# Attention computed head by head with 1024-column exponentials, in place of pairs of heads with 512-column ones

## The reference, cut to what matters

```python
xh  = x.reshape(b, c, h, he).transpose(0, 2, 1, 3)      # c = 2048 tokens, h = 16, he = 64
qkv = einsum('bhce,ef->bhcf', xh, Wqkv) + bqkv
q, k, v = split(qkv, 3, axis=-1)
att = einsum('bhqe,bhke->bhqk', q, k) / sqrt(he)
mask = tril(ones((c, c)), k=-1)
att = softmax(att * mask, axis=-1)      # masked scores are 0, not -inf: they count as exp(0) = 1
out = einsum('bhqk,bhke->bhqe', att, v)
x = x + (out @ Wr + br)                 # x was layer-normed before attention
x = x + moe(layernorm(x))               # 1 shared + 8 routed experts, D=1024, H=2048
```

## Time and profile before

| | us |
|---|---|
| two timed runs | 4086.95 and 4326.6, median 4206.77 |
| the profiled run's own time | 4113.86 |
| its span, slowest core (core 3) | 4112.3 |
| its span, fastest core (core 0) | 3973.3 |
| TensorE busy on core 3 | 3071.2 (75%) |
| DVE busy | 1200.4 (29%) |
| ACT busy | 869.4 (21%) |

### The profile page before, as it was taken

How to read it: one execution, slowest core, us unless ns; L and a number is a source line. 1 busy time by engine, 2 the same in 40 slices (tenths; PEclk the granted TensorE clock), 3 DMA queues, 4 the chain that set the end, 5 groups by cost and what they waited for, 6 DMA issues and landing times.

```text
span 4112.3 us, 45933 instructions; the slowest of 8 cores (3973.3 to 4112.3 us)
## 1 busy us (share of the span) xinstructions
PE 3071.2 (75%) x15380; PEld 1367.7 (33%) x15380; DVE 1200.4 (29%) x2450; ACT 869.4 (21%) x1354; POOL 29.2 (1%) x55
## 2 busy tenths in 40 slices
PE   2354445554545445837999999999999999999997
PEld 0122222222222222313444444344444444444343
DVE  5222222222222222361132323223332232323222
ACT  0232323232323223002211121211212211121210
POOL 0000000000000000000000000000000000000000
PEclk7555555555555555868988999889998888999888
DMA  2100000000000000040040222204022040222202
GB/s 83 26 1 1 1 1 1 1 1 1 1 1 1 1 1 1 1 83 1 11 72 1 41 42 42 42 1 83 1 41 42 11 72 1 42 42 42 42 1 82
DMA packets 7087, 98.28 MB, mean 24 GB/s; under 512 B 1860, under 2 KB 2260, under 8 KB 2388
## 3 DMA queue, kind: packets, MB, share of 16 engines
q0 software_dynamic: 3984, 77.81, 11.2%
q1 hardware_dynamic: 2884, 17.53, 1.3%
HBM read 164.58 MB, written 8.39 MB: 42 GB/s over the span
## 4 chain that ended last, share of the span: by engine, by line
PE 68%; DVE 13%; ACT 8%; issue 8%; DMA 1%; DVEq 1%; ACTq 0%; SPq 0%; POOL 0%
PE PM L771 27%; PE PM L860 26%; PE PS L460 6%; DVE SMASK L433 4%; PE PS L409 3%; ACT PTE L422 3%; ACT PTO L439 2%; ACT PTE L439 2%; PE PTR L492 2%; DVE AVN L485 2%; PE PS L533 1%; DVE RZ L480 1%; PE PS L383 1%; PE PS L374 1%; DVE TMPLN L243 1%
## 5 line engine op out<-in xcount | busy, mean ns | idle before, releaser
L771 PE MATMUL PM<-XLN,W 128*128 128x512 bf16 x4608 | 1100.3, 406 | 0.7 <-DVE WSB L729 0.7
L860 PE MATMUL PM<-H1G,W 128*128 128x512 bf16 x4608 | 1058.9, 395 | 0.0
L788 ACT ACTIVATE H1G<-PM,B1C 128x512 bf16<-128x512 f32 x576 | 395.9, 687 | 1750.9 <-PE PM L771 1750.9
L771 PEld LDWEIGHTS PM<-XLN,W 128*128 128x128 bf16 x4608 | 473.8, 103 | 623.6 <-issue 304.7
L860 PEld LDWEIGHTS PM<-H1G,W 128*128 128x128 bf16 x4608 | 464.9, 101 | 589.5 <-issue 196.9
L409 PE MATMUL PS<-QT,KT 64*128 64x512 bf16 x640 | 345.0, 582 | 258.5 <-DVE SMASK L433 171.5
L837 DVE TENSOR_TENSOR H1G<-H1G,WB 128x512 bf16<-128x512 bf16 x512 | 217.7, 425 | 765.7 <-ACT H1G L788 765.7
L875 DVE TENSOR_TENSOR XRES<-XRES,PM 128x512 f32<-128x512 f32 x288 | 198.2, 688 | 709.5 <-PE PM L860 709.5
L492 PE MATMUL PTR<-IDB,AVN 128*64 128x128 bf16 x256 | 68.8, 269 | 351.3 <-DVE AVN L485 351.3
L433 DVE TENSOR_TENSOR SMASK<-PS,MASKS 128x512 f32<-128x512 f32 x256 | 177.1, 692 | 480.4 <-PE PS L409 378.2
L409 PEld LDWEIGHTS PS<-QT,KT 64*128 64x128 bf16 x640 | 64.9, 101 | 526.8 <-issue 520.5
(11 more groups left out here) (102 smaller groups left out, 1149.0 us busy)
## 6 DMA issues: line engine op xcount, KB each, us to landing
W<-w1cat POOLq DMA_DIRECT2D x9, 4096.0 KB, 28.6
W<-w2cat POOLq DMA_DIRECT2D x9, 4096.0 KB, 28.5
XRES<-xt SPq DMA_DIRECT2D x8, 1024.0 KB
ot<-XRES SPq DMA_DIRECT2D x8, 1024.0 KB
WRF<-wr_rl POOLq DMA_DIRECT2D x1, 2048.0 KB, 17.0
MASKS<-c_masks SPq DMA_DIRECT2D x1, 512.0 KB
B1C<-b1col POOLq DMA_DIRECT2D x9, 8.0 KB, 27.9
B2C<-b2col_t POOLq DMA_DIRECT2D x9, 4.0 KB, 3.2
```

The costliest lines, as they stand in the source:

```text
L771: lambda e, psv=psv, kc=kc, ht=ht, tt=tt: e.matmul(psv, W1[:, kc * DFF + ht * 128: kc * DFF + (ht + 1) * 128], xln(kc)[:, tt * 512:(tt + 1 ...
L788: lambda e, h1sl=h1sl, psv=psv, e_i=e_i, ht=ht: e.activation(h1sl, psv, AF.Gelu, bias=B1C[:, (e_i % 2) * 16 + ht: (e_i % 2) * 16 + ht + 1]),
L860: lambda e, psv=psv, kc=kc, dtl=dtl, buf=buf: e.matmul(psv, W2[:, kc * D + dtl * 128: kc * D + (dtl + 1) * 128], H1G[:, buf * 8192 + kc * 512:
```

## The change

Each head is now worked on by itself.

- Q and K: one 64-row matmul and one eviction for each slot, in four banks of PS4; a matmul of the third and fourth token tile waits for the eviction two tiles before it. QT and KT have 64 partitions, VA one head. Every head lies in partitions 0 to 63 of QT and KT.
- V: as before for one head; its first matmul waits for PS2, which Q and K no longer use. The first score matmul waits for the Q/K evictions only, the AV matmuls for the copy of V.
- Unmasked scores: two key tiles of one head fill two neighbouring banks, and one exponential reads 1024 columns. Its event goes to `sc_hist` twice.
- Masked scores: two masks, each 512 columns, fill both halves of SMASK, both after the preceding exponential; one exponential of 1024 columns follows. Each mask's event goes to `sc_hist`.
- AV: once for each head and block, then the same four steps, but reciprocal and scaling read PS1 in PSUM; the copy to PAVS is gone. PS1 comes free with the last copy into AVT.
- The mask constant is float32 and so twice as large.

```diff
-    c_masks = dt("c_masks", [128, 4 * 512], BF16, kind="ExternalInput").ap()
+    c_masks = dt("c_masks", [128, 4 * 512], F32, kind="ExternalInput").ap()
...
-                for hp in range((min(H, DBG["nheads"]) + 1) // 2):
...
+                for h in range(min(H, DBG["nheads"])):
+                    ch, off = h // 2, (h % 2) * 64
...
+                            if s >= 2:
+                                w = [("SS", evs[s - 2])]
+                            else:
+                                w = [slot_free[slot_id]]
...
+                            tq = P.emit("tensor",
+                                        lambda e, psv=psv, wcol=wcol, tsl=tsl, xh=xh,
+                                        off=off: e.matmul(
+                                            psv, WQ[off:off + 64, wcol:wcol + 64],
+                                            xh[:, tsl],
+                                            start=True, stop=True),
+                                        waits=w, inc="ST")
...
+                        for kc0 in range(0, 4 * j, 2):
+                            slot = rot % 6
+                            rot += 2
...
+                            for q in range(2):
+                                kc = kc0 + q
+                                psv = base[:, boff + q * 512: boff + (q + 1) * 512]
+                                w = [slot_free[slot + q]]
                                 if len(sc_hist) >= 2:
                                     w.append(sc_hist[-2])
...
+                            ss_exp_last = P.emit("scalar",
+                                    lambda e, base=base, boff=boff, kc0=kc0: e.activation(
+                                        PT[:, kc0 * 512:(kc0 + 2) * 512],
+                                        base[:, boff:boff + 1024],
+                                        AF.Exp, scale=0.125),
+                                    waits=[("ST", ts)] + ptguard, inc="SS")
+                            slot_free[slot] = ("SS", ss_exp_last)
+                            slot_free[slot + 1] = ("SS", ss_exp_last)
+                            sc_hist.append(("SS", ss_exp_last))
+                            sc_hist.append(("SS", ss_exp_last))
+                        for kc0 in range(4 * j, 4 * j + 4, 2):
...
+                                vm = P.emit("vector",
+                                        lambda e, psv=psv, d=d, q=q: e.tensor_mul(
+                                            SMASK[:, q * 512:(q + 1) * 512],
+                                            psv, MASKS[:, d * 512:(d + 1) * 512]),
+                                        waits=[("ST", ts), ("SQ", sq_masks),
+                                               ("SS", ss_exp_last)], inc="SV")
+                                slot_free[slot + q] = ("SV", vm)
+                                sc_hist.append(("SV", vm))
...
+                            ss_exp_last = P.emit("scalar",
+                                    lambda e, kc0=kc0: e.activation(
+                                        PT[:, kc0 * 512:(kc0 + 2) * 512],
+                                        SMASK[:, 0:1024],
+                                        AF.Exp, scale=0.125),
+                                    waits=[("SV", vm)] + ptguard, inc="SS")
...
-                            pcp = P.emit("vector",
-                                    lambda e: e.tensor_copy(PAVS[:, 0:260], PS1[:, 0:260]),
-                                    waits=[("ST", st_av), ("SV", ps1_free[1])], inc="SV")
-                            ps1_free = ("SV", pcp)
...
+                                        RZ[:, mt:mt + 1],
+                                        PS1[:, mt * 65 + 64: mt * 65 + 65]),
...
+                                        AVN[:, mt * 64:(mt + 1) * 64],
+                                        PS1[:, mt * 65: mt * 65 + 64],
+                                        RZ[:, mt:mt + 1], None, ALU.mult),
...
+                        ps1_free = ("SV", avt_done)
```

More of the change, by code:

```diff
@@ L315, in build_program @@
                 avt_done = 0
[L317 to L322, removed]
-                for hp in range((min(H, DBG["nheads"]) + 1) // 2):
[L325 to L336, removed]
-                                w += [("SV", ln1_done), ("GQ", gq_wq)]
[L338 to L392, removed]
@@ L393, in build_program @@
                                        PS2.ap().rearrange("p (g n) -> p g n", n=64)),
                                    waits=[("ST", tv_last), ("SV", sv_vones)], inc="SV")
-                        ps2_free = ("SV", sv_va[oh])
-                    for j in range(NTT):
[L397 to L403, removed]
+                    else:
+                        sv_va = sv_vones
@@ new lines, in build_program @@
+                                            KT[0:64, kc * 128:(kc + 1) * 128],
+                                            QT[0:64, j * 512:(j + 1) * 512],
+                                            start=True, stop=True),
+                                        waits=w, inc="ST") or ts
+                            ptguard = [("ST", st_av_prev)] if kc0 == 0 else []
+                            ss_exp_last = P.emit("scalar",
[4 more added lines that the diff above has]
+                                    waits=[("ST", ts)] + ptguard, inc="SS")
@@ new lines, in build_program @@
+                            slot_free[slot] = ("SS", ss_exp_last)
[3 more added lines that the diff above has]
+                        for kc0 in range(4 * j, 4 * j + 4, 2):
+                            slot = rot % 6
+                            rot += 2
+                            base = (PS4 if slot < 4 else PS2)
+                            boff = (slot if slot < 4 else slot - 4) * 512
+                            vm = 0
+                            for q in range(2):
+                                kc = kc0 + q
+                                psv = base[:, boff + q * 512: boff + (q + 1) * 512]
+                                w = [slot_free[slot + q]]
+                                if len(sc_hist) >= 2:
+                                    w.append(sc_hist[-2])
+                                if kc == 0 and j == 0:
+                                    w += [("SS", ev_q[-1]), ("SS", ev_k[-1])]
+                                ts = P.emit("tensor",
+                                        lambda e, psv=psv, kc=kc, j=j: e.matmul(
+                                            psv,
+                                            KT[0:64, kc * 128:(kc + 1) * 128],
+                                            QT[0:64, j * 512:(j + 1) * 512],
+                                            start=True, stop=True),
+                                        waits=w, inc="ST")
+                                d = kc - 4 * j
+                                vm = P.emit("vector",
[6 more added lines that the diff above has]
+                                sc_hist.append(("SV", vm))
+                            ptguard = [("ST", st_av_prev)] if kc0 == 0 else []
+                            ss_exp_last = P.emit("scalar",
[4 more added lines that the diff above has]
+                                    waits=[("SV", vm)] + ptguard, inc="SS")
@@ new lines, in build_program @@
+                        st_av = 0
+                        for mt in range(4):
+                            for kc in range(16):
+                                if kc < 4 * j + 4:
+                                    lhs = PT[:, kc * 512 + mt * 128: kc * 512 + (mt + 1) * 128]
+                                else:
+                                    lhs = ONES[:, 0:128]
+                                w = []
+                                if mt == 0 and kc == 0:
+                                    w = [("SS", ss_exp_last), ("SV", sv_va), ps1_free]
+                                st_av = P.emit("tensor",
+                                        lambda e, lhs=lhs, mt=mt, kc=kc: e.matmul(
+                                            PS1[:, mt * 65:(mt + 1) * 65],
+                                            lhs, VA[:, kc * 65:(kc + 1) * 65],
+                                            start=(mt == 0 and kc == 0), stop=(kc == 15),
+                                            skip_group_check=True),
+                                        waits=w,
+                                        inc=("ST" if (mt == 3 and kc == 15) else None)) or st_av
@@ L514, in build_program @@
+                        ps1_free = ("SV", avt_done)
+                        if h == 0 and j == 0:
+                            _DBGREF["PT"] = PT
+                            _DBGREF["AVN"] = AVN
+                            _ckpt("j0")
                 _DBGREF["AVT"] = AVT
```

204 lines of the change are left out of this document (93 added, 111 removed).

## The result

The changed kernel takes 4182.6 us (median of 11 runs), the kernel before 4130.3 (10 runs). Some executions are held back on part of the cores by a lower clock; the ratio of those that aren't is 1.0194, with a 95% interval from 1.0105 to 1.0283. So after is slower, by about what was summed (1.8%): the interval excludes 1, but leaves open whether it is more or less than 2%. The profiled execution of after took 4128.1 us, its slowest core 4126.6.

A forecast was written before the change was run, and what follows sets the result against it. Attention was taken as a chain with one engine working at a time, so its length counts. Terms of +98, -26 and +2 gave +74 us on 4112.3, then 1.6 for the profiled run: 4188 us, range 4135 to 4250.

The forecast's parts named there:

- Unmasked cycle: Unmasked scores: two matmuls, then one 1024-column exponential, 2.28 us against 1.42 before; 192 pairs, +165 us.
- Masked pair: Masked scores: two masks, then one exponential, 2.56 us against 3.04 before; 128 pairs, -61 us.
- Both with Q/K/V: Q/K/V and all score blocks: 61.9 us per head, 990 us for 16 heads against 892 before, +98 us.
- Normalisation: After AV: dropping the copy to PAVS saves 34 us, less the cost of PSUM reads; -26 us.
- Loading the masks: Start of kernel: masks load as 1024 KB, not 512, beside the WRF load before the first Q matmul; +2 us.
- The rival of dear PSUM reads: Normalisation: reads from PSUM 65 ns slower eat 33 of the 34 us saved; 4213 us, chance 0.15.
- The clock rival: Score blocks: clock rises to 2.4 GHz, a cycle loses 0.39 us; no change, about 4113 us, chance 0.05.
- The other rivals: Slower matmuls and masks, no copy saving, up to 4258 us (0.10); TensorE a pair ahead, 3950 (0.04); chain unlengthened, 4115 (0.04).
- The sign: Whole kernel: chances of slower 0.45, faster 0.04, within 2% 0.51, with 82 us taken as the measurable limit.

The follow-up runs named there:

- e3: Changed kernel with unmasked exponentials of 512 columns again, one per matmul, each with its own history entry; attention 1445.6 us, 165.1 less than the changed kernel.
- e6: Changed kernel with masked items one by one again (mask, 512-column exponential, next mask waits); attention 1675.2 us, 64.5 more than the changed kernel.
- e4: Changed kernel with one history entry, not two, for each unmasked exponential; attention 1408.1 us, 202.6 less than the changed kernel.
- e7: Changed kernel with the mask in bf16 again; attention 1611.4 us against 1610.7, first Q matmul at 129.1 us against 130.9.
- e1: Changed kernel with score matmuls waiting only for their banks, not the history list; attention 1373.2 us.
- e9: The changed kernel itself again, five rounds beside the kernel before; ratio 1.0125, from 1.0033 to 1.0218.

## Why the prediction was right, and where it was wrong

**The time and its mechanism: right.** 4188 us were predicted, 4182.6 measured. That the two lie within 6 us is in part luck: the executions of after lie at 4128, 4155, 4183 and above, by what clock the expert part got, and attention grew by 66 us where the sum has 72 for it. Step by step:

- *Unmasked cycle.* 0.43 + 0.68 + 1.03 + 0.14 = 2.28 us; measured 2.27. The exponential of 1024 columns takes 1.024 us, and the second matmul starts 0.43 behind the first as assumed (1.01 for two of 0.58). +165 us; e3 takes this edit back and gets 165.1.
- *Masked pair.* 2.56 against 2.54; the guess of 0.60 between two independent masks held. -61 us; e6 measured -64.5.
- *Both with Q/K/V.* 990 us after; the table gives 990.2. Before, 892 were summed from units and 894.9 measured, so the difference was 95 and not 98. Inside this sum Q/K/V was mis-sized in detail. I took 0.71 us from eviction to eviction; with one 64-row eviction to a bank they follow at 0.57 (332.01, 332.59, 333.16 in core 3's timeline), so a head needs 9.06 us to its first score matmul. The first mask waits for the copy of V in both readings, which is why little of it reached the sum: the copy starts when V is done. That the 990 is met so closely is luck in part: Q/K/V with j=0 measured 253 us where the sum has 16 x 16.26 = 260, and j=1 to 3 measured 737 where it has 730.
- *Normalisation.* -26 predicted, -30.8 measured. The price of reading PSUM was right (0.13 against 0.14 us a block). What was missing: the first DVE instruction starts 0.08 us earlier after AV (3.86 us behind the group's start in the earlier trace rows's block, 3.78 in e4). 64 x 0.08 = 5 us. The old copy waited for two semaphores and the reciprocal waits for one, which may be the cause; no run tests it alone.
- *Loading the masks.* +2 predicted; the first Q matmul starts 1.4 us later in the median over the cores, and 1.8 against e7.
- *The rival of dear PSUM reads* (0.15) is refuted by the 284 and 161 ns. So is, here, the Trainium skill's pair of fixed costs (VectorE: DVE Perf Modes, The TRN2 errata) as a forecast of this saving: 30 and 4 ns more were measured where its difference of 62 cycles gives an estimate of 65. The clock rival is refuted too: cycles at 2.27 us are those of 1.2 GHz, and the clock line reads 5 through attention in both profiles (0.54 on average from 110 to 1690 us of core 3, in both). The other rivals are out as well: the matmul is 0.43 and the mask 0.60 behind the one before it, and attention grew by 66 us. Of the rule of the Trainium skill (TensorEngine Tiling (Array Packing), Tiling Modes), e3 shows that the lost parallelism of array halves lies off the chain.

**The sign: wrong.** The likeliest case in my chances was "within 2%" (0.51), against 0.45 for slower, while my own sum said 1.8% slower. The step that failed is not a term of the sum but the sentence that about 2%, 82 us, is what a measurement of this kernel can tell from no change. It rested on no row: the prediction gives no reason for it, and the scatter that it names, two runs 240 us apart and cores 139 us apart, is not the error of a ratio over many runs. In its place the runs showed an interval of +-0.9% from ten and eleven runs, and two independent sets (1.0194 and 1.0125) both exclude 1. An effect of 65 to 68 us was measurable, and a sum of +74 with errors of some 30 should have been called "slower" first. The second weakness was not to use a gauge that the trace offers: attention by itself repeats within 3 us.

**The noise, on the other hand, was named rightly.** "139 us depend on what clock the expert part gets" is what separates the cores. From the last transpose to the end, the cores of before, after and most experiments take 2297 to 2303 us, or 2327, 2355, 2382, 2410, 2438: steps of 28 us. (e1 has values off these steps, 2311, 2314 and 2454, which I can't explain.) A part of the windows view of before, core 3, shows most of one such stretch and a later part without one (window, its length, then busy time and count of each engine, granted clock, DMA share, GB/s):

```profile
2130.00:2290.00 160.00, 160.00 (x620) 66.73 (x619) 42.46 (x78) 30.93 (x45) 0.00 (x0) 0.83 0.02 4
...
2385.00:2605.00 220.00, 215.10 (x985) 96.52 (x984) 73.94 (x127) 39.90 (x58) 2.67 (x5) 0.98 0.18 32
```

The first window catches the end of the stretch: in windows of 20 us the clock reads 0.81 from about 2100 to 2266 us and 1.00 on either side, though TensorE is busy throughout. An estimate of the loss is 160 x (1 - 0.81) = 30 us; the cores' differences say 28. Read in this way, core 3 of before has five such stretches, core 3 of after three, and core 3 of e9 none, as many as it has steps. The two cores of a pair (0 and 1, 2 and 3, and so on) always have the same number: their spans differ by less than 8 us in every execution on record. Five stretches against three are why the two profiled spans differ by only 14 us.

**What stays open.** Why single evictions follow at 0.57 us and paired ones at 0.71 was not tested; two evictions of a pair read one bank, single ones different banks, but that is only an argument. What decides how many slow stretches a pair of cores gets was not tested either, nor why DVE starts 0.08 us earlier after AV.

## What to carry to other kernels

When two instructions are merged into one, the waits that count entries ("the one before last") change their meaning: here the same list and the same index went from two items ahead to none. Check how far each engine may run ahead before pricing the saved overhead; here the wide instruction was worth 0.05 us a pair, and with the lost depth a pair took 0.86 more than two narrow items. And where the span mixes a steady part with one whose clock varies, measure the changed stage alone, and don't call an effect unmeasurable from the scatter of two runs.

## What the runs showed that I had not expected

- The experts' part of a core loses time in whole steps of about 28 us, each one stretch of about 160 us at a clock of 0.81, while other pairs of cores of the same die and run have none. The Trainium skill (TensorE: Matmul & The Clock Gate, Seeing it yourself) describes a third level of 13/16 that takes a whole die under dense work on several of its cores and holds while the load lasts. The trace agrees in size (0.81), but not in the rest: these stretches end after some 160 us and come again, or not, and in before cores 2 and 3 have five while cores 0 and 1 of their die have none.
- Evictions of 64 partitions: 0.57 us apart singly, 0.71 in pairs, at an unchanged duration of 0.68.
- One pair of run-ahead was not enough for ACT's pace: 1.14 us a pair in e4, 0.91 in e1, though TensorE's 0.86 us of matmuls (2 x 0.43) fit under one exponential: it is the round trip of 2.28 us, shared by two pairs, that sets this pace.
